# Second attention of a two-layer gated cross-attention and expert block: jobs of the queries and of the output placed in other steps of a hand-written order

## The reference, cut to what matters

```python
q = (x @ Wq + bq).reshape(1, B * N, H, hd)          # 2048 rows, 16 heads of 16
q = _fq_sym(q * scale, axis=-1)                      # 8-bit levels per row and head
k = _fq_sym(k, axis=-1); v = _fq_sym(v, axis=2)      # 512 context rows
attn = softmax(einsum('bhqd,bhkd->bhqk', q, k))
attn = _fq_unsigned(attn, axis=-1)                   # 255 levels
out = einsum('bhqk,bhkd->bhqd', attn, v) @ Wp + bp
x = x + tanh(g_xattn[1]) * out
```

## Time and profile before

| | |
|---|---|
| time of three runs | 951.81, 952.78, 956.13 us; median 952.78 |
| the profiled execution | 959.28 us, of which the span between first and last instruction is 957.5 |
| busy in the span | PE 746.1 us, DVE 686.8, POOL 505.3, PEld 496.1, ACT 443.4 |
| granted TensorE clock, mean | 0.843 of full speed |
| the attention's steps | maxima (L1450) start from 375.2 to 620.4 us of the span |

### The profile page before, as it was taken

How to read it: one execution, slowest core, us unless ns; L and a number is a source line. 1 busy time by engine, 2 the same in 40 slices (tenths; PEclk the granted TensorE clock), 3 DMA queues, 4 the chain that set the end, 5 groups by cost and what they waited for, 6 DMA issues and landing times.

```text
span 957.5 us, 18420 instructions
## 1 busy us (share of the span) xinstructions
PE 746.1 (78%) x5700; PEld 496.1 (52%) x5701; DVE 686.8 (72%) x1825; ACT 443.4 (46%) x1037; POOL 505.3 (53%) x607
## 2 busy tenths in 40 slices
PE   3469749678988797677777777659879999977994
PEld 1258635456664454344444444335657777754563
DVE  4868947756775777988887888738857777734467
ACT  3355335123332233888887878725123444422331
POOL 6284974566636557553554347010054545478883
PEclk9679876789999899697767676657979999978998
DMA  8034444624542213898889988821034444446444
GB/s 287 1 92 157 157 157 147 187 80 142 164 127 89 66 34 81 146 191 160 151 163 168 182 159 162 148 75 40 0 93 137 136 136 140 142 123 143 79 79 141
DMA packets 205754, 121.17 MB, mean 127 GB/s; under 512 B 146476, under 2 KB 197808, under 8 KB 205680
## 3 DMA queue, kind: packets, MB, share of 16 engines
q1 hardware_dynamic: 192816, 91.10, 39.2%
q0 software_dynamic: 12864, 29.14, 12.5%
HBM read 64.16 MB, written 32.98 MB: 101 GB/s over the span
## 4 chain that ended last, share of the span: by engine, by line
PE 35%; DVE 11%; ACT 7%; issue 6%; DVEq 4%; DMA 3%; another core or an unknown queue 2%; POOL 1%; POOLq 0%; ACTq 0%
PE PS L269 18%; PE PS L852 4%; DVE sb_wk L1450 4%; PE PS L791 3%; ACT sb_xnf L1417 3%; DMA sb_xnf<-sb_xnf 3%; PE PS L1344 2%; ACT sb_wkh L1417 2%; PE PS L815 2%; PE PS L844 2%; PE PS L407 1%; DVEq L250 1%; DVE sb_x_sb L942 1%; DVE sb_x_sb L948 1%
## 5 line engine op out<-in xcount | busy, mean ns | idle before, releaser
L673 POOL DMA_INDIRECT sb_xnf<-token_table,sb_ids x120 | 115.8, 965 | 148.7 <-DVE sb_wk L1018 62.8
L1450 DVE TENSOR_SCALAR_CACHE_REDUCE sb_wk<-PS 128x512 f16<-128x512 f32 x256 | 161.9, 684 | 3.8 <-PE PS L1344 3.8
L269 PE MATMUL PS<-sb_xnT,sb_sgu 128*128 128x512 f16 x528 | 129.5, 398 | 1.1 <-DVE sb_lg L455 0.6
L269 PE MATMUL PS<-sb_region,sb_wkh 128*128 x720 | 122.6, 321 | 4.8 <-issue 3.1
L1417 ACT ACTIVATE sb_xnf<-PS,sb_slotv 128x512 int16<-128x512 f32 x128 | 86.8, 689 | 25.5 <-DVE sb_wk L1450 21.4
L875 ACT ACTIVATE sb_wk<-PS 128x512 f32<-128x512 f32 (+1 forms) x48 | 28.6, 596 | 144.6 <-PE PS L269 123.7
L269 PEld LDWEIGHTS PS<-sb_region,sb_wkh 128*128 128x128 f16 x720 | 69.7, 100 | 47.0 <-issue 13.9
L1417 ACT ACTIVATE sb_wkh<-PS,sb_slotv 128x512 int16<-128x512 f32 x128 | 86.6, 690 | 12.4 <-DVE sb_wk L1450 9.6
L852 PE MATMUL PS<-sb_region,sb_wkh 128*128 x600 | 78.3, 277 | 8.9 <-DVE sb_wa L1031 7.3
L269 PEld LDWEIGHTS PS<-sb_xnT,sb_sgu 128*128 128x128 f16 x528 | 53.0, 102 | 60.7 <-issue 10.9
L791 PE MATMUL PS<-sb_sdn,sb_wkh 128*128 128x256 f16 x544 | 70.8, 282 | 17.4 <-DVE sb_wkh L989 15.2
(11 more groups left out here) (296 smaller groups left out, 1717.3 us busy)
## 6 DMA issues: line engine op xcount, KB each, us to landing
slot_table<-sb_wa SPq DMA_DIRECT2D x60, 256.0 KB
slot_table<-token_table SPq DMA_DIRECT2D x16, 640.0 KB
sb_stg<-gu SPq DMA_DIRECT2D x24, 352.0 KB
sb_stg<-dn SPq DMA_DIRECT2D x24, 256.0 KB
token_table<-sb_xnf SPq DMA_DIRECT2D x16, 256.0 KB, 4.7
sb_stg<-sgu SPq DMA_DIRECT2D x8, 352.0 KB
sb_x_sb<-x SPq DMA_DIRECT2D x1, 2048.0 KB, 12.3
out<-sb_x_sb SPq DMA_DIRECT2D x16, 128.0 KB
```

Source lines behind the costliest of these rows:

```text
L269: last = nc.tensor.matmul(out_, lhs(i, c), rhs(j, c), start=(c == 0 and n == 0 and not begun), stop=(c == C - 1 and n == 2 and not more))
L673: nc.gpsimd.indirect_dma_start(xg[l][:, 2 * (g % XR) + n, :], None, xw[l][:, :], bass.IndirectOffsetOnAxis(ap=ids[:, 2 * g + n:2 * g + n + ...
L1450: nc.vector.tensor_scalar(h_any[(2 * s + h) % 6], PS[:, (2 * s + h) % LB, :], LEVELS, None, ALU.add, ALU.min, accum_out=h_nb[s % 3][:, h:h ...
```

## The change

Jobs of the side work are given other steps. Nothing is added to or removed from what is computed.

```diff
-        ROWS, TO_PE, HIGH_Q, LOW_Q, PRODUCTS, LARGEST, SCALES, FRACTIONS, PARTS, BACK, COPIES = 0, 1, 2, 3, 4, 7, 8, 10, 10, 12, 13
+        ROWS, TO_PE, HIGH_Q, LOW_Q, PRODUCTS, LARGEST, SCALES, FRACTIONS, PARTS, BACK, COPIES = 0, 1, 1, 4, 3, 7, 8, 10, 10, 10, 11
 
         def chain_start(G):
 
-            return max((GSTEPS - 1) * (G - 1), GSTEPS * (G - 1) - 4)
+            return max((GSTEPS - 2) * (G - 1), GSTEPS * (G - 1) - 4)
...
-                o = output_step(s, 6)
+                o = output_step(s, 5)
                 if o is not None:
                     output_transposes(o)
                 for j in range(2):
-                    o = output_step(s, 8 + j)
+                    o = output_step(s, 7 + j)
                     if o is not None:
                         project(o, j)
...
-                o = output_step(s, 6)
+                o = output_step(s, 5)
                 if o is not None:
                     output_high(o)
...
-                o = output_step(s, 7)
+                o = output_step(s, 8)
                 if o is not None:
                     output_low(o)
-                o = output_step(s, 10)
+                o = output_step(s, 11)
                 if o is not None:
                     update(o)
                 for j in range(2):
-                    o = output_step(s, 11 + j)
+                    o = output_step(s, 12 + 3 * j)
                     if o is not None:
                         stats(2 * o + j)
```

## The result

The changed kernel takes 970.33 us, median of 4 runs (968.54 to 970.61); the kernel before, on the same chip, 952.29 us (951.72 to 956.13). The ratio is 1.0177, 95% interval 1.0147 to 1.0206: slower by 1.8%. The forecast was 963.6 us, range 948 to 977, and slower with a chance of 0.65.

A forecast was written before the change was run, and what follows sets the result against it. No engine was full; DVE, busy 184.0 of 219.0 us, was nearest to the bound. Terms 9.9 + 0 + 0 + 3 - 2.1 gave +10.8 us on 952.78, so 963.6 us, range 948 to 977.

The forecast's parts named there:

- parts 1 and 2: Output's shift and earlier transposes back, over six rounds with both kinds of side work: +9.9 us, bounds +3.6 and +18.
- part 5: Group 1, without output work: too few maxima cover the wait for the transposes back; +3 us.
- part 6: The last round, with output work alone: DVE idles less, -2.1 us.
- parts 3 and 4: Queries' low part and products (0, bounds -5 and +5); queries' high part in PE's own step (0, bounds 0 and 2.5).
- the deciding part: Transposes back two steps earlier, fractions left at 10: PE waits 3.6 us for POOL; a round loses 0.6, 1.6 or 3.0.
- The sign: PE's transposes L1253 wait for POOL seven times for 3 to 3.6 us; less than 1 us a time would refute.
- the faster rival: PE comes late enough at the transposes back, POOL is finished, removed waits stay gone: -10 us, 942; chance 0.12.
- the low case: Low clock through a round's transposes and projections: DVE idles 2.2, 1.4 and 2.2, together 5.8 us; round loses 3.0.
- The mixed case: First transposes and projection at low clock, second at high: DVE idles 2.2 + 1.4 + 0.8 = 4.4 us; round loses 1.6.
- the low-clock rival: Low clock through the whole burst, second transposes and projection slow as well: +24.7 us, 977; chance 0.15.
- Part 1: Output's low part and update later, projection earlier: waits of 6.1 and 15.4 go; first product loses 1.1 low, 0.1 high.
- Part 7: Earlier group starts and copies, later second statistics, transposing DMAs in order: cost nothing.

The follow-up runs named there:

- Part 3 alone: The kernel before with the queries' low part at 4 and products at 3 and 4, high part left at 2: 959.82 us, ratio 1.0041.
- Part 4 alone: The kernel before with only the queries' high part on ACT at 1 for 2: 960.63 us, ratio 1.0035.
- The last kernel: The new placement with the queries' low part at 4 in place of 3: 933.19 us, ratio 0.9763 to the kernel before.
- the output shift: The kernel before with the output's jobs alone as in the change (projection 7 and 8, low part 8, update 11): 948.49 us, ratio 0.9931.
- the new placement: The kernel before with output transposes 5, high part 6, low part 8, projection 8 and 9, update 11, statistics 12 and 15: 939.09 us, ratio 0.9816.

## Why the prediction was right, point by point

**The sum, term by term, in the changed kernel itself.** The sum can be set beside DVE's waits in front of the maxima in the changed kernel's trace (41.4 us from 402 to 634), taken round by round, less the waits that stood there before (29.6 us).

| term | put on record | before | after | measured |
|---|---|---|---|---|
| parts 1 and 2, the output's half of six rounds | +9.9 | 16.9 | 24.9 | +8.0 |
| part 5, group 1 | +3 | 0 | 3.0 | +3.0 |
| part 6, the last round | -2.1 | 4.6 | 2.9 | -1.7 |
| parts 3 and 4, the queries' half | 0 | 8.1 | 10.5 | +2.4 |
| together, before rounding | +10.8 | 29.6 | 41.4 | +11.8 |

Ahead of 402 us, at group 1's products, the waits grew by another 1.1 us (0.96 + 1.14 against 0.63 + 0.42), which also belongs to parts 3 and 4. That makes 12.9 of the 13.8 us by which the loop is longer. So each term has the right sign or was small, and two sizes were off in opposite ways: the deciding part by 1.9 us too dear, parts 3 and 4 by 3.5 too cheap. That these partly cancel is luck; the mechanism is not.

**The deciding part (2) was right in mechanism and nearly in size.** In the round that was worked out, PE was to stand 3.6 us and then DVE idle 2.2 + 1.4 + 0.8 = 4.4; the trace has 2.96 and 2.17 + 1.25 + 1.28 = 4.7. PE stood less because it came later: ACT's high part, now at place 5, lay right ahead of the exponentials of place 6 (519.11, then 519.60), and PE waited 1.14 us for one of them at 520.43. The sign was too bold: it had seven waits of 3 to 3.6 us, and only one of the seven first waits reached 3. Group 2's, 0.24, was even under the 1 us that was to refute it; there PE came late enough, which is the faster rival in one round of seven. Undoing the part gives back 1.7%, the whole loss.

**The clock went between the mixed and the low case.** In the round shown the first transposes take 1.03 and the first projection 1.44, as at the low level. The second transposes still take 1.01, where the earlier trace rows have 0.61, and only the second projection, 0.98, is on its way from the 1.2 to the 2.4 GHz level. Idle at place 11 is 1.28, between the 0.8 of the mixed and the 2.2 of the low case. Over the rounds the second transposes take 0.62, 0.61, 0.85, 1.01, 1.01 and 1.01 us. The mixed case thus fits the earlier rounds, and the later ones drew nearer the low-clock rival, whose full price (1.4 and 2.2 us in place of 1.25 and 1.28) did not come about. The Trainium skill, "TensorE: Matmul & The Clock Gate", section "HAM oscillation — how this bites in real kernels", has bursts after a wait begin slow; the trace agrees for the start of each burst, 1.03 and 1.44 us, and the burst ends faster, 0.98 us.

**Parts 3 and 4 were the terms that were mis-sized.** Both were priced at 0. In the changed kernel they cost 2.4 + 1.1 = 3.5 us by the waits; alone in the kernel before they cost 9 us, 1.0095, just beyond their two bounds together (5 + 2.5). Part 3 alone, 1.0041 or 3.9 us, lies inside its bound. Part 4 alone, 1.0035 or 3.3 us, has an interval of 1.1 to 5.7 us, so it is not 0, and whether it passed its bound of 2.5 cannot be told. It was costed by the output's high part, whose wait in DVE's row was 0.35. But the cost of a wait in ACT is not only the wait of the job that follows it: it is also the late exponential, which shows as a wait for logits under another name.

**Part 1** was carried inside the rounds' sum. Alone it is a gain of 6.6 us, of the size of its own working. The waits of L269 for L1465 and L1271, about 1 us each by the sign, are there when the part stands alone (5.4 us in six waits for L1465), but in the changed kernel only one of 1.4 and four of at most 0.4 are left, since PE now comes late to them from its stand in front of the transposes (525.90, with the low part done by 523.4).

**Part 7** put the earlier copies at nothing. ACT waits 18.9 us for them, and in the round shown above this holds nothing up. No run moved the copies apart from the transposes, so it is shown for that round only.

**The faster rival** named waits that could be removed; with the transposes back at 12 that became 1.0006 and not 942 us. The other parts explain it: parts 3 and 4 ate what part 1 gave (0.9931 x 1.0095 = 1.0025).

**Parts 1 and 2 do not add.** The transposes back alone cost 2.9%, on top of the rest of the change 1.7%, because the output's transposes stand behind or ahead of the stall.

**The last difference.** The profiled executions differ by 11.3 us, near the forecast's 10.8, but the medians by 18.0. The closeness of the first is in part luck, since the kernel before was profiled in an execution slower than the four timed beside the change. It gave 952.3 in that comparison and 956.2 to 957.5 in later ones, so part of the 18.0 lies in its spread; how much was not tried, since the changed kernel was not timed again.

## What to carry to other kernels

In an order written out by hand, a job's place has to be judged on every engine: moving VectorE's job away from what it waits for can be worth nothing if the next engine's job is moved towards what that one waits for, and each hand-over of a chain (also the one through an engine that has no steps of its own, GpSimd here with 4.25 us) needs its distance. Before moving a job, take from the trace how long after its producer's end it starts now; here the transposes had 0.9 us of margin and were moved by two steps. Of the waits inside one step, ScalarE's for TensorE are easily overlooked: the job behind it hardly waits, and yet the queries' high part one step earlier cost 0.35%, which shows as waits for logits.

## What the runs showed of the hardware that was not expected

The last kernel has a DMA share of 1.02 in the stretch from 402 to 600 us (0.92 before), of transfers that no engine's row shows as busy. In that kernel ACT waits 8.5 us for the transposing ones there, where it was 5.0 before. Whether they are the next bound no run shows:

```profile
ACT sb_xnf L1417 <- DMA sb_xnf<-sb_xnf: 4.5, 6, 1.6
ACT sb_wkh L1417 <- DMA sb_wkh<-sb_wkh: 4.0, 5, 1.6
```

And with fewer stalls the granted clock was higher: 0.80 in that stretch against 0.74 before (0.78 in the output shift, 0.80 in the new placement), so the 2.4 GHz level was granted more of the time. Part of the gain may thus come through faster matmuls; how much of this kernel's 2.4% it is was not tried.
